# Scores of odd heads in banks of their own, in the single-piece steps of a causal attention

## The chip, the cores and the metric

The kernel runs on the 8 cores of one Trainium2 chip. Each core computes 2 of the 16 sequences of the batch, with all weights, and the cores exchange nothing. The metric is the device time in microseconds (us) of the slowest core.

## What is computed

One pre-norm transformer block: causal attention with 16 heads of 64, then a gated feed-forward part with two hidden 4096 x 4096 layers. Per core 2 sequences of 2048 tokens, width 1024.

```python
# x: (16, 2048, 1024), layernorm without gain and bias
qkv  = jnp.einsum('btc,hdc->bhtd', layernorm(x), w_qkv); q, k, v = jnp.split(qkv, 3, axis=-1)
dots = jnp.einsum('bhtd,bhsd->bhts', q, k) * hs ** (-0.5)
dots = jnp.where(causal, dots, -jnp.inf)
out  = jnp.einsum('bhts,bhsd->bhtd', jax.nn.softmax(dots, axis=-1), v)
x = x + out.transpose(0, 2, 1, 3).reshape(Bx, Tx, -1) @ w_proj.T + b_proj
y = layernorm(x)
h = silu((y @ w1.T) * w1_s) * ((y @ w2.T) * w2_s)
h = gelu((h @ h1.T) * h1_s);  h = gelu((h @ h2.T) * h2_s)
x = x + (h @ w3.T) * w3_s
```

## The kernel before

Each core runs attention for its first sequence, then for its second, then four feed-forward sweeps of 1024 tokens. Every instruction is put into one of five engine queues when the program is built. An engine works through its queue in order. An instruction carries the semaphore values that it waits for. On VectorE and ScalarE each instruction also waits for the one before it on the same engine.

**Attention** of one sequence: layernorm and transposes of 16 token tiles (lines 310 to 360), projections to Q, K and V for eight pairs of heads (L401 to L434), and then the steps: 16 query tiles of 128 queries (`qt`) times 16 heads (`h_`), heads innermost. A step of query tile `qt` has K = (qt+1)·128 keys. PSUM has 8 banks of 512 fp32 columns. Banks 0 to 3 take the scores, in pieces of 1024 columns (two banks), banks 4 and 5 the transposed probabilities, banks 6 and 7 the output of all heads of a tile. Query tiles 0 to 7 have up to 1024 keys and so one piece ("single-piece"), tiles 8 to 15 have two.

The parts of a step:

- `emit_qpad`: ScalarE copies the head's 64 rows of Q into one of two zero-padded buffers (L464), by the parity of the head.
- `emit_S_mm`: PE computes the scores, one matmul per 512 keys (L490). VectorE takes the negated maximum of a full first piece (L499, two-piece steps only), adds the causal mask to the last 128 columns (L504), takes the negated maximum of the last piece (L509), and joins the two (L513, two-piece only).
- `emit_exps`: ScalarE writes the exponential to SBUF with a running sum (L530, ACTIVATE and the read of the accumulator). VectorE copies the sum (L547), or adds the two of a two-piece step (L543). `gbank` of the score banks is set to the exponential: it is what the next score matmul into the bank waits for. `expg[par]` does the same for mask and maximum, by the parity of the head.
- `emit_PTAV`: for each group of four key blocks of 128, PE transposes the probabilities into bank 4 or 5 (L566). ScalarE (even groups, L576) or VectorE (odd groups, L579) copies them to SBUF, and PE multiplies them with V (L593). Steps of up to 512 keys have one group, those of 640 to 1024 keys two.
- `emit_tail`: after the last head of a query tile, scaling (L611, L618), transposes (L626), the output projection (L643), bias and residual (L652, L655) and the store.

The order of the emission is one head ahead: scores, mask and maximum of step i, the Q copy of step i+1, transposes and AV of step i-1 (and the tail, if that was the tile's last head), then the exponential of step i:

```python
for idx, (qt, h_) in enumerate(seq):
    nmx, vred = emit_S_mm(qt, h_)
    if idx + 1 < len(seq):
        emit_qpad(*seq[idx + 1])
    if pend is not None:
        emit_PTAV(*pend)
        if pend[1] == H - 1:
            emit_tail(pend[0])
    cev_ = emit_exps(qt, h_, nmx, vred)
```

So PE's queue holds scores of i, transposes of i-1, AV of i-1, scores of i+1. VectorE's holds mask and maximum of i, the L579 copy of i-1, L547 of i, mask of i+1. ScalarE's holds the Q copy for i+1, the L576 copy of i-1, the exponential of i.

**The feed-forward sweeps**: each has the gate and up matmuls (L767, 1024 of 512 columns), two hidden layers (L812, 2048 matmuls each) and the output layer (L851), with the weights streamed in from scratch copies in HBM that GpSimd's queue cast to bf16 during the first attention.

Of the kernel before, what the change touches and what calls it, by code (L numbers as in the profile page):

```python
# [69 lines left out]
def ceil_div(a, b):  # L70
    return (a + b - 1) // b


def build(cfg):
# [108 lines left out]
    PS = ps_t.ap()  # L183

    def sb(off, n, dtype=BF16, parts=(0, 128)):
        if dtype == BF16:
            v = A[parts[0]:parts[1], off // 2: off // 2 + n]
        else:
            v = A[parts[0]:parts[1], off // 2: off // 2 + 2 * n].bitcast(F32)
        return v  # L190

    def bank(i, w=512):
        return PS[:, i * 512: i * 512 + w]
# [5 lines left out]
    mtri = sb(o_binT, 128)  # L199
# [24 lines left out]
    s_exp = s_wt = s_e  # L224
    prog.self_sem = {"vector": v_e, "scalar": s_e}

    gbank = {i: None for i in range(8)}
    tw_lane = [0, 0]

    def em(eng, fn, wait=(), inc=None, inc_n=1):  # L230
        return prog.emit(eng, fn, wait, inc, inc_n)
# [134 lines left out]
    def attention(b):  # L366
# [15 lines left out]
        for hp in range(NHP):  # L382
# [9 lines left out]
            for part, dsto, evac_eng in ((0, o_Q, "scalar"), (1, o_K, "vector")):  # L392
                for tt in range(NT5):
                    bk = part * 2 + (tt % 2) if False else (0 if part == 0 else 1)
                    bk = (tt % 2) + (0 if part == 0 else 2)
                    for cc in range(NCC):
# [5 lines left out]
                               o, l, r, start=st_, stop=sp),  # L402
# [15 lines left out]
            for sc_ in range(T // 128):  # L418
                bk = 4 + (sc_ % 2)
                for cc in range(NCC):  # L420
# [5 lines left out]
                           o, l, r, start=st_, stop=sp),  # L426
# [41 lines left out]
        def emit_S_mm(qt, h_):  # L468
            K_ = (qt + 1) * 128
            npiece = ceil_div(K_, 1024)  # L470
            qtw = qt * 128
            pd = qtw // 1024
            hp, lo = h_ // 2, (h_ % 2) * 64
            hpv = hp * T
            par = h_ % 2
            nm = sb(o_nmp + par * 16, 4, F32)
            qp = (o_qpad // 2) + par * 128
            qpad_ev = qpad_evs[par]
            ts_p = []
            for p in range(npiece):  # L480
                w_p = min(1024, K_ - p * 1024)
                for jj in range(ceil_div(w_p, 512)):
                    w_j = min(512, w_p - jj * 512)
                    bk = 2 * p + jj
                    off = p * 1024 + jj * 512
                    lhs = A[:, qp: qp + 128]
                    rhs = A[:, (o_K // 2) + hpv + off:
                            (o_K // 2) + hpv + off + w_j]
                    em("tensor", lambda t, o=bank(bk, w_j), l=lhs, r=rhs:
                       t.matmul(o, l, r, start=True, stop=True),  # L490
                       wait=(gbank[bk], qpad_ev,
                             qkv_done_v if qt == 0 and h_ == 0 else None,
                             qkv_done_s if qt == 0 and h_ == 0 else None),
                       inc=t_s if jj == ceil_div(w_p, 512) - 1 else None)
                ts_p.append((t_s, t_s.v))
                if p < pd:
                    em("vector", lambda v, o=nm[:, p:p + 1],
                       i_=PS[:, p * 1024: p * 1024 + 1024]:
                       v.tensor_reduce(out=o, in_=i_, axis=AX.X, op=ALU.max,  # L499
                                       negate=True),  # L500
                       wait=(ts_p[p], expg[h_ % 2]))
            qpad_guard[par] = (t_s, t_s.v)
            em("vector", lambda v, o=PS[:, qtw: qtw + 128], m=mtri:
               v.tensor_tensor(out=o, in0=o, in1=m, op=ALU.add),  # L504
               wait=(ts_p[pd], expg[h_ % 2]))
            w_pd = K_ - pd * 1024
            em("vector", lambda v, o=nm[:, pd:pd + 1],
               i_=PS[:, pd * 1024: pd * 1024 + w_pd]:
               v.tensor_reduce(out=o, in_=i_, axis=AX.X, op=ALU.max,  # L509
                               negate=True))  # L510
            if npiece > 1:
                em("vector", lambda v, o=nm[:, 3:4], i_=nm[:, 0:npiece]:
                   v.tensor_reduce(out=o, in_=i_, axis=AX.X, op=ALU.min,  # L513
                                   negate=False))
            nmx = nm[:, 3:4] if npiece > 1 else nm[:, 0:1]
            return nmx, (v_e, v_e.v)

        def emit_exps(qt, h_, nmx, vred):
            K_ = (qt + 1) * 128
            nsc = qt + 1  # L520
            par = h_ % 2
            Poff = (o_P // 2) + par * T
            rsp = sb(o_rsp + par * 16, 4, F32)
            nj = ceil_div(K_, 1024)
            chunk_ev = {}
            for j in range(nj):
                w_j = min(1024, K_ - j * 1024)
                em("scalar", lambda sc, o=A[:, Poff + j * 1024: Poff + j * 1024 + w_j],
                   i_=PS[:, j * 1024: j * 1024 + w_j], bi=nmx, a=rsp[:, j:j + 1]:
                   sc.activation(out=o, in_=i_, func=AF.Exp, bias=bi, scale=1.0,  # L530
                                 accum_out=a),
                   wait=(vred, hpar_guard[par] if j == 0 else None,
                         rsg[par] if j == 0 else None),
                   inc=s_exp)
                for sc_ in range(j * 8, min(j * 8 + 8, nsc)):
                    chunk_ev[sc_] = (s_exp, s_exp.v)
                gbank[2 * j] = (s_exp, s_exp.v)
                gbank[2 * j + 1] = (s_exp, s_exp.v)
            expg[par] = (s_exp, s_exp.v)
            rs = sb(o_rs, H, F32)  # L540
            if nj > 1:
                em("vector", lambda v, o=rs[:, h_:h_ + 1], i_=rsp[:, 0:nj]:
                   v.tensor_reduce(out=o, in_=i_, axis=AX.X, op=ALU.add),  # L543
                   wait=(expg[par],), inc=v_e)
            else:
                em("vector", lambda v, o=rs[:, h_:h_ + 1], i_=rsp[:, 0:1]:
                   v.tensor_copy(o, i_), wait=(expg[par],), inc=v_e)  # L547
            rsg[par] = (v_e, v_e.v)
            return chunk_ev
# [126 lines left out]
# [9 lines that stand above are left out]
            pend = (qt, h_, cev_)  # L685
# [311 lines left out]
```

How the kernel before makes its waits and increments, by code:

```python
def build(cfg):  # L74
# [830 lines left out]
    gbank[("xF", 1)] = x1_stores_done  # L905
    gbank[("x2F", 0)] = x1_stores_done
    gbank[("x2F", 1)] = x1_stores_done
    t0 = 0
    for si, SW in enumerate(sweeps):
        ffn_sweep(si, t0, SW)
        t0 += SW
    final_st = d_st.v
    em("sync", lambda s: s.wait_ge(d_st.h, final_st))
    with nc.Block() as block:
        def run(eng_name):
            def _(eng):
                for waits, fn, inc, inc_n in prog.q[eng_name]:
                    for s, v in waits:
                        eng.wait_ge(s.h, v)
                    inst = fn(eng)
                    if inc is not None:
                        inst.then_inc(inc.h, inc_n)
```

## Time and profile before

| | |
|---|---|
| median of 3 runs | 8859.74 us (8769.2 to 9204.07) |
| profiled execution | 8801.45 us |
| span of its slowest core (core 2) | 8799.8 us |
| spans of the others | 8734.7 to 8790.0 us |
| PE, DVE, ACT busy | 79%, 20%, 23% of the span |
| mean granted TensorE clock, core 2 | 0.834 |
| attention of the first and second sequence | to about 1848 and 3493 us, the rest is feed-forward |

Times in the rows are us from the span's start. PE is TensorE's matmuls, PEld its weight loads, DVE VectorE, ACT ScalarE, POOL GpSimd. The granted clock (PEclk) is a share of 2.4 GHz, so 0.50 is 1.2 GHz. L490 is line 490 of the kernel. All rows are of core 2.

### The profile page before, as it was taken

The numbers are of one execution on the slowest core, as the hardware profiler recorded it, in microseconds if no ns is written. First come the engines' busy times: TensorE is split into PE (matmuls) and PEld (weight loads), VectorE is DVE, ScalarE is ACT, GpSimd is POOL, SyncE is SP. The second block draws the span as 40 slices with busy tenths as digits, with TensorE's granted clock in tenths as the row PEclk, the third lists the DMA queues.
The fourth block names the chain that finished last, engine by engine and source line by source line (L and its number), as shares of the span: only waits on it lengthen the run. The fifth ranks groups of instructions, "written<-read, shape, count | busy, mean of one in ns | idle before, by whom it ended". The sixth has DMA issues, their size and how long they took to land.

```text
span 8799.8 us, 101925 instructions; the slowest of 8 cores (8734.7 to 8799.8 us)
## 1 busy us (share of the span) xinstructions
PE 6972.6 (79%) x37120; PEld 3410.8 (39%) x37120; DVE 1802.5 (20%) x3585; ACT 2024.7 (23%) x3840; POOL 191.9 (2%) x142
## 2 busy tenths in 40 slices
PE   0645556657455665999997999996999996999998
PEld 0423333334233333444443444443444443444443
DVE  1234445543344455200000200001200001100000
ACT  0034455532445554210000210000210000110000
POOL 1000000100000000000000000000000000000000
PEclk9965555668555565999998999998999998899999
DMA  5987777531000000333336333335333335333335
GB/s 78 94 83 76 77 72 73 57 61 26 20 15 11 10 11 22 77 79 76 76 77 140 73 79 77 77 76 140 71 78 77 77 77 139 59 77 76 76 77 129
DMA packets 2139544, 626.25 MB, mean 71 GB/s; under 512 B 2114224, under 2 KB 2114352, under 8 KB 2139056
## 3 DMA queue, kind: packets, MB, share of 16 engines
q1 hardware_dynamic: 1649184, 417.41, 23.7%
q0 software_dynamic: 461216, 101.00, 13.4%
q10 hardware_dynamic: 28656, 101.34, 3.5%
q8 instruction: 306, 5.01, 0.3%
q14 instruction: 182, 1.49, 0.1%
HBM read 269.23 MB, written 134.22 MB: 46 GB/s over the span
## 4 chain that ended last, share of the span: by engine, by line
PE 67%; DVE 12%; issue 7%; DMA 7%; ACT 6%; DVEq 1%; ACTq 1%; SPq 0%; POOLq 0%
PE ps L812 40%; PE ps L767 11%; PE ps L851 4%; PE ps L490 4%; DVE arena L509 4%; ACT arena L530 4%; PE ps L401 3%; DVE arena L499 2%; DMA arena<-x_scratch 2%; PE ps L643 2%; DMA qkvB<-wqkv 2%; DVE ps L504 1%; ACT arena L576 1%; DMA arena<-w3B 1%; PE ps L566 1%
## 5 line engine op out<-in xcount | busy, mean ns | idle before, releaser
L812 PE MATMUL ps<-arena 128*128 128x512 bf16 x16384 | 3537.5, 379 | 9.0 <-DVE arena L790 5.1
L812 PEld LDWEIGHTS ps<-arena 128*128 128x128 bf16 x16384 | 1602.6, 98 | 1944.0 <-issue 12.7
L825 ACT ACTIVATE arena<-ps,arena 128x512 bf16<-128x512 f32 x512 | 351.7, 687 | 3158.8 <-PE ps L812 3158.8
L593 PE MATMUL ps<-arena 128*128 128x64 bf16 x4352 | 402.6, 228 | 719.2 <-DVE arena L579 400.4
L767 PE MATMUL ps<-arena 128*128 128x512 bf16 x4096 | 930.4, 393 | 0.0
L885 DVE TENSOR_TENSOR arena<-ps,arena 128x1024 f32<-128x1024 f32 x32 | 39.2, 1224 | 4155.8 <-DMA arena<-x_scratch 4155.8
L490 PE MATMUL ps<-arena 128*128 128x512 bf16 (+3 forms) x1280 | 541.1, 531 | 351.0 <-ACT arena L530 347.5
L530 ACT ACTIVATE arena<-ps,arena 128x1024 bf16<-128x1024 f32 (+7 forms) x768 | 663.9, 864 | 439.9 <-DVE arena L655 259.5
L593 PEld LDWEIGHTS ps<-arena 128*128 128x128 bf16 x4352 | 268.8, 115 | 927.7 <-issue 927.3
L566 PE MATMUL ps<-arena 128*128 128x128 bf16 x4352 | 624.4, 305 | 0.0
L767 PEld LDWEIGHTS ps<-arena 128*128 128x128 bf16 x4096 | 411.7, 101 | 517.2 <-issue 141.0
L576 ACT COPY arena<-ps 128x512 bf16<-128x512 bf16 (+3 forms) x768 | 408.3, 532 | 783.8 <-PE ps L566 783.8
L566 PEld LDWEIGHTS ps<-arena 128*128 128x128 bf16 x4352 | 476.0, 142 | 142.5 <-issue 130.8
L851 PE MATMUL ps<-arena 128*128 128x512 bf16 x2048 | 455.8, 384 | 18.0 <-DMA arena<-w3B 14.0
L509 DVE TENSOR_REDUCE arena<-ps 128x1 f32<-128x512 f32 (+7 forms) x512 | 388.0, 758 | 54.8 <-DVE ps L504 1.6
L790 DVE SCALAR_TENSOR_TENSOR arena<-ps,arena 128x512 bf16<-128x512 f32 x256 | 192.1, 751 | 746.8 <-PE ps L767 746.8
L783 ACT ACTIVATE arena<-ps,arena 128x512 bf16<-128x512 f32 x256 | 175.9, 687 | 726.0 <-PE ps L767 725.5
L348 PE MATMUL ps<-arena 128*128 128x128 bf16 x512 | 63.3, 307 | 350.8 <-DVE arena L339 327.5
L401 PE MATMUL ps<-arena 128*128 128x512 bf16 x1024 | 227.8, 384 | 142.0 <-DMA arena<-qkvB 140.7
L499 DVE TENSOR_REDUCE arena<-ps 128x1 f32<-128x1024 f32 x256 | 313.5, 1224 | 62.3 <-PE ps L490 47.9
L490 PEld LDWEIGHTS ps<-arena 128*128 128x128 bf16 x1280 | 102.3, 106 | 572.1 <-issue 567.7
L851 PEld LDWEIGHTS ps<-arena 128*128 128x128 bf16 x2048 | 200.5, 99 | 272.1 <-issue 50.2
(51 smaller groups left out, 2371.4 us busy)
## 6 DMA issues: line engine op xcount, KB each, us to landing
arena<-x ACTq DMA_DIRECT2D x64, 512.0 KB, 4.5
h1B<-h POOLq DMA_DIRECT2D x32, 1024.0 KB, 16.3
h2B<-h POOLq DMA_DIRECT2D x32, 1024.0 KB, 15.9
arena<-x_scratch ACTq DMA_DIRECT2D x64, 512.0 KB, 4.2
x_scratch<-arena ACTq DMA_DIRECT2D x32, 512.0 KB, 2.8
out<-arena ACTq DMA_DIRECT2D x32, 512.0 KB, 3.0
w1B<-w POOLq DMA_DIRECT2D x8, 1024.0 KB, 18.8
w2B<-w POOLq DMA_DIRECT2D x8, 1024.0 KB, 16.1
```

Of the source, the lines that this page charges most:

```text
L401: st_=(cc == 0), sp=(cc == NCC - 1): t.matmul(o, l, r, start=st_, stop=sp),
L490: t.matmul(o, l, r, start=True, stop=True),
L499: v.tensor_reduce(out=o, in_=i_, axis=AX.X, op=ALU.max, negate=True),
L509: v.tensor_reduce(out=o, in_=i_, axis=AX.X, op=ALU.max, negate=True))
L530: sc.activation(out=o, in_=i_, func=AF.Exp, bias=bi, scale=1.0, accum_out=a),
L566: em("tensor", lambda t, o=outb, i_=inb: t.transpose(o, i_, ident), wait=(chunk_ev[sc_] if (idx == 0 or sc_ == qt) else None, gbank[("pt", ...
L576: em("scalar", lambda sc, d=dstv, s=srcv: sc.copy(d, s), wait=(tpt, gbank[("PT", slot)]), inc=csem)
L593: st_=(sc_ == 0), sp=(sc_ == nsc - 1): t.matmul(o, l, r, start=st_, stop=sp),
L767: st_=(cc == 0), sp=(cc == NCC - 1): t.matmul(o, l, r, start=st_, stop=sp),
L812: st_=(dc == 0), sp=(dc == ND - 1): t.matmul(o, l, r, start=st_, stop=sp),
L825: s1=scalev[:, oc:oc + 1]: sc.activation(out=o, in_=i_, func=AF.Gelu, scale=s1),
L851: st_=(dc == 0), sp=(dc == ND - 1): t.matmul(o, l, r, start=st_, stop=sp),
```

## The change

In single-piece steps the scores of odd heads go to PSUM columns 1024 to 2047 (banks 2 and 3), those of even heads stay in columns 0 to 1023 (banks 0 and 1). The offset `sbase` is added where the scores are written, masked, reduced, exponentiated, and where the bank guards are set. In two-piece steps `sbase` is 0 and nothing changes. No instruction is added or removed, and the order of the queues is the same.

```diff
@@ emit_S_mm
+            sbase = par * 1024 if npiece == 1 else 0
             ...
-                    bk = 2 * p + jj
+                    bk = sbase // 512 + 2 * p + jj
             ...
-                       i_=PS[:, p * 1024: p * 1024 + 1024]:
+                       i_=PS[:, sbase + p * 1024: sbase + p * 1024 + 1024]:
             ...
-            em("vector", lambda v, o=PS[:, qtw: qtw + 128], m=mtri:
+            em("vector", lambda v, o=PS[:, sbase + qtw: sbase + qtw + 128], m=mtri:
             ...
-               i_=PS[:, pd * 1024: pd * 1024 + w_pd]:
+               i_=PS[:, sbase + pd * 1024: sbase + pd * 1024 + w_pd]:
@@ emit_exps
+            sbase = par * 1024 if nj == 1 else 0
             ...
-                   i_=PS[:, j * 1024: j * 1024 + w_j], bi=nmx, a=rsp[:, j:j + 1]:
+                   i_=PS[:, sbase + j * 1024: sbase + j * 1024 + w_j], bi=nmx,
+                   a=rsp[:, j:j + 1]:
             ...
-                gbank[2 * j] = (s_exp, s_exp.v)
-                gbank[2 * j + 1] = (s_exp, s_exp.v)
+                gbank[sbase // 512 + 2 * j] = (s_exp, s_exp.v)
+                gbank[sbase // 512 + 2 * j + 1] = (s_exp, s_exp.v)
```

## Rows read from the trace of the kernel before

**Rows 1.** The page, part 4: the chain that ended last, by line.
```profile
PE ps L812 40%; PE ps L767 11%; PE ps L851 4%; PE ps L490 4%; DVE arena L509 4%; ACT arena L530 4%; PE ps L401 3%; DVE arena L499 2%; DMA arena<-x_scratch 2%; PE ps L643 2%; DMA qkvB<-wqkv 2%; DVE ps L504 1%; ACT arena L576 1%; DMA arena<-w3B 1%; PE ps L566 1%
```

**Rows 2.** Groups by line and shape, 0 to 3600 us: busy us, mean ns | idle before.
```profile
L547 DVE COPY arena<-arena 128x1 f32<-128x1 f32 x256 | 39.4, 154 | 254.3 <-ACT arena L530 249.0 <-ACT arena L464 5.3
...
L579 DVE COPY arena<-ps 128x128 bf16<-128x128 bf16 x64 | 14.4, 224 | 28.1 <-PE ps L566 24.8
```

**Rows 3.** Timeline, one step with 1024 keys: start, us, engine line operation [idle before].
```profile
940.82 1.11 ACT L530 ACTIVATE arena<-ps,arena 128x1024 bf16<-128x1024 f32 x1 [0.74 <-DVE arena L509]
...
942.17 1.01 PE L490 MATMUL ps<-arena 128*128 128x512 bf16 x2 [0.45 <-ACT arena L530]
942.19 0.15 DVE L547 COPY arena<-arena 128x1 f32<-128x1 f32 x1 [1.00 <-ACT arena L530]
...
942.98 1.06 PE L566 MATMUL ps<-arena 128*128 128x128 bf16 x8
...
943.36 0.30 DVE L504 TENSOR_TENSOR ps<-ps,arena 128x128 f32<-128x128 f32 x1 [1.01 <-PE ps L490]
943.76 1.23 DVE L509 TENSOR_REDUCE arena<-ps 128x1 f32<-128x1024 f32 x1
943.81 0.58 ACT L576 COPY arena<-ps 128x512 bf16<-128x512 bf16 x1 [1.40 <-PE ps L566]
...
945.09 0.42 DVE L579 COPY arena<-ps 128x512 bf16<-128x512 bf16 x1
945.13 1.11 ACT L530 ACTIVATE arena<-ps,arena 128x1024 bf16<-128x1024 f32 x1 [0.74 <-DVE arena L509]
...
945.66 0.37 PE L593 MATMUL ps<-arena 128*128 128x64 bf16 x4 [0.75 <-DVE arena L579]
```

**Rows 4.** Timeline, one step with 256 keys.
```profile
529.37 0.47 ACT L530 ACTIVATE arena<-ps,arena 128x256 bf16<-128x256 f32 x1 [0.37 <-DVE arena L509]
...
530.08 0.37 PE L490 MATMUL ps<-arena 128*128 128x256 bf16 x1 [0.66 <-ACT arena L530]
...
530.11 0.15 DVE L547 COPY arena<-arena 128x1 f32<-128x1 f32 x1 [0.89 <-ACT arena L530]
...
530.63 0.30 DVE L504 TENSOR_TENSOR ps<-ps,arena 128x128 f32<-128x128 f32 x1 [0.37 <-PE ps L490]
...
531.03 0.42 DVE L509 TENSOR_REDUCE arena<-ps 128x1 f32<-128x256 f32 x1
...
531.61 0.47 ACT L530 ACTIVATE arena<-ps,arena 128x256 bf16<-128x256 f32 x1 [0.36 <-DVE arena L509]
```

**Rows 5.** Windows: busy us (instructions) by engine, PEclk, DMA share, GB/s.
```profile
901.00:966.00 65.00, 38.37 (x262) 22.84 (x262) 30.55 (x59) 31.28 (x60) 6.31 (x4) 0.50 0.76 73
...
1520.00:1580.00 60.00, 39.17 (x310) 23.26 (x308) 33.48 (x69) 36.03 (x69) 6.31 (x4) 0.61 0.66 59
```

**Rows 6.** Timeline, end of a step of the last, two-piece query tile.
```profile
1776.12 1.11 ACT L530 ACTIVATE arena<-ps,arena 128x1024 bf16<-128x1024 f32 x1
...
1776.57 0.37 PE L593 MATMUL ps<-arena 128*128 128x64 bf16 x4 [0.53 <-DVE arena L579]
...
1776.76 1.47 PE L490 MATMUL ps<-arena 128*128 128x512 bf16 x3
```

**Rows 7.** Timeline, L547 in another step with 256 keys.
```profile
523.38 0.15 DVE L547 COPY arena<-arena 128x1 f32<-128x1 f32 x1 [1.24 <-ACT arena L464]
```

**Rows 8.** The chain of work in order of time, attention's end: start, us, what.
```profile
3492.64 2.61 DMA x_scratch<-arena
3495.79 6.45 DMA arena<-x_scratch
```

**Rows 9.** The chain, L767 of the third and fourth sweep, and a window in the latter.
```profile
6168.66 222.05 PE ps L767 x1024
...
7487.00 262.71 PE ps L767 x1024
...
7507.00:7527.00 20.00, 20.00 (x78) 8.30 (x77) 3.00 (x4) 3.73 (x6) 0.00 (x0) 0.81 0.33 66
```

## Prediction

> **What bounds the kernel now.** I read the page's chain of work first: the feed-forward line L812 holds 40% of it, and the lines of the softmax steps (L490, L509, L530, L499) about 4%, 4%, 4% and 2% [rows 1]. The change touches only those, so it works inside the attention part, and there only in the steps of the first eight query tiles, whose scores fit into two PSUM banks. The grouped view gives their number: L547 runs in these steps alone, 256 times (8 tiles x 16 heads x 2 batches) [rows 2]. The same row shows VectorE idle for 254.3 us ahead of it, 249.0 us of that until the exponential of the same head was done.
>
> Then I read the timeline of single steps, one large and one small. With 1,024 keys a step repeats every 4.31 us (940.82 to 945.13). The reader should follow one chain through it: exponential L530 starts at 940.82; its accumulator is read out 1.35 us later and at 942.17 the two score matmuls L490 start on the banks just freed; the mask add L504 starts 1.19 us after them, the maximum L509 0.40 us after that, runs 1.23 us, and the next exponential starts 0.14 us behind it [rows 3]. With 256 keys it is the same chain: 0.71 + 0.55 + 0.40 + 0.58 = 2.24 us (529.37 to 531.61) [rows 4]. No engine is full; a ring of waits through ACT, PE and DVE sets the pace. The granted clock is 0.50 in such a stretch, which is the level of 1.2 GHz [rows 5].
>
> **The change, part by part.** Nothing is computed more or less, no DMA is touched, no wait is added. Odd heads of single-piece steps put their scores at column 1,024 of PSUM, so in banks 2 and 3, and mask, maximum and exponential follow. The guard of the score matmul of head h+1 becomes the exponential of head h-1, long done, instead of that of head h. The bookkeeping costs nothing: every instruction keeps its size and engine. What is worth time is how early L490 of head h+1 can start now, and what is late next. All queues keep their order, so two waits take over.
>
> The first is on VectorE. Its queue holds, between the maximum of head h and the mask of head h+1, the copy L547, which waits for the exponential of head h. Mask and maximum therefore can't run beside that exponential; only the score matmul can. Before, L547 started 0.02 to 0.03 us after L490 (942.19 against 942.17, 530.11 against 530.08). After, the mask starts behind L547: its 0.15 us and 0.11 us from one VectorE instruction's end to the next one's start (943.76+1.23 to 945.09 shows 0.10) [rows 3, 4]. The stretch from L490 to L504 (1.19 us with 1,024 keys, 0.55 with 256) shrinks to 0.02 or 0.03 + 0.26. That saves 0.91 and 0.26 us. Between them it grows by (1.19-0.55)/6 = 0.107 us for each 128 keys. I call this loop B. Its savings by keys, 128 to 1,024: 0.16, 0.26, 0.37, 0.48, 0.58, 0.69, 0.80, 0.91.
>
> The Trainium skill (PSUM — Partial Sum Buffer, section Engine vs sequencer instructions) says that the VectorE and ScalarE queues are strictly first in, first out. It speaks against reading the change as full overlap of two heads, and the trace agrees, with 249.0 us of such waiting at L547. Could the mask pass L547, at most 0.26 us more would be saved in each of the 128 steps of up to 512 keys, 33 us, and the time would be 8655.
>
> The second wait exists from 640 keys on, where a step has a second group of transposes. Its copy L579 is on VectorE behind the maximum, the AV matmuls L593 wait for the copy, and L490 of the next head is behind these on PE. Loop C with 1,024 keys: 0.10 from the maximum's end to L579 (944.99 to 945.09), 0.42 copy, 0.15 to L593 (945.51 to 945.66), then L593 to L490, 1.19 to the mask, 0.40 to the maximum, 1.23 maximum [rows 3]. L593 to L490 doesn't occur unblocked in these steps. The nearest row is in the last tile of the batch: L593 at 1776.57, L490 at 1776.76, so 0.19 us [rows 6]. Bounds: 0, since it can't start ahead of it; and 0.37 + 0.15 = 0.52, if it waited for L593's end (0.37) and one hand-over more. I take 0.19, as it is the same pair of lines. Loop C is 3.68 us then, against 4.31: 0.63 saved, less than loop B's 0.91, so C decides. With 640 keys: the step before is 2.24 + 3 x 0.345 = 3.28 (0.345 is (4.31-2.24)/6); C is 0.10 + 0.22 + 0.15 + 0.19 + 0.87 + 0.40 + 0.83 = 2.76, with the copy from the grouped rows [rows 2] and the maximum between 0.42 and 1.23 [rows 3, 4]; 0.52 saved, under B's 0.58. Between them 0.55 and 0.59.
>
> ScalarE has a ring of its own: exponential, transposes, copy L576, next exponential. With 512 keys: 0.92 us to the transposes (between 0.71 and 1.35), 0.83 to the copy (942.98 to 943.81), 0.58 copy, 0.10 to the next: 2.43 [rows 3, 4]. The step in loop B is 2.24 + 2 x 0.345 - 0.48 = 2.45. It lies just behind and doesn't decide.
>
> Sum for the eight tiles: 0.16 + 0.26 + 0.37 + 0.48 + 0.52 + 0.55 + 0.59 + 0.63 = 3.56 us per head; x 16 heads x 2 batches = 114 us. That takes the step across a tile's end (projection, residual) for one like the others: the score matmul of the next tile's first head is moved in the same way. Nothing catches up the gain: the chain goes from the last tile's store to the loads of the feed-forward part, with no wait for weights between [rows 8]. The profiled execution took 8801.45 us; 8801.45 - 114 = 8687. This execution lies between the runs shown (8769.2 and the median 8859.74), so a median may come out up to 50 us higher.
>
> Bounds of the sum: with 0.52 for L593 to L490 each large step saves 0.33 less: 64 x 2 x 0.33 = 42 us, so 72 us and 8729. With 0 each large step saves 0.19 more, capped by loop B: 1.27 + 0.58 + 0.69 + 0.78 + 0.82 = 4.14 us, x 32 = 132 us, 8669.
>
> **Rivals.** *The clock rises.* PE's work of a step would stand closer together. In a stretch of the later tiles, where it does so too, the granted clock is 0.61, so partly the level of 2.4 GHz [rows 5]. At that level L490 and the transposes halve, loop C drops below B, and B holds everywhere: 4.25 x 32 = 136 us, 8665. Against it: most of that stretch stays at 1.2 GHz as well, and all of the one with 1,024 keys. The Trainium skill (TensorE: Matmul & The Clock Gate, Part 1) says that the gate follows how busy PE has been, two levels and none between; the mean of 0.61 fits a mixture.
>
> *A late release takes the place.* L547 now is on the path, and it isn't always let go at once: at 523.38 VectorE had been idle for 1.24 us ahead of it, where the regular step has 0.89 [rows 4, 7]. Before, the score matmul hid this. If each step lost these 0.35 us, loop B would save 0, 0, 0.02, 0.13, 0.23, 0.34, 0.45, 0.56: 1.73 x 32 = 55 us, 8746. Against it: almost all of the steps in the trace are regular.
>
> *It doesn't do what it says.* PE now writes scores while ScalarE reads the other head's. If the exponential were held up for as long as the matmul streams (0.107 us per 128 columns, 36 x 0.107 = 3.85 us over the eight sizes), of loop B's 4.25 us only 0.40 x 32 = 13 us would be left: 8788. Against it: in a two-piece step the exponential of 1776.12 takes 1.11 us with L490 of 1776.76 beside it, as long as the one of 940.82 with no L490 beside it [rows 3, 6].
>
> *Slower than before: the granted clock of the feed-forward part.* On core 2 the L767 stage took 222.05 us in the third sweep and 262.71 in the fourth, whose stretch from 7507 shows a granted clock of 0.81 [rows 9]. Place: the dense matmul stages, which the change shifts in time against those of the other cores. Price: 40.7/222 = 18% of each stage so affected. It decides from 114/0.18 = 620 us of such stages more than now. If one sweep's three long stages fell into it (222 us and two of the eight L812 stages, which share 40% of the span, so 440 us each [rows 1, 9]), that is 1102 us and 18% of it: 8687 + 202 = 8889. Against it: one stage of a fourth of the sweeps shows it, and nothing ties it to attention. The Trainium skill (same page, Part 1) describes a current limit of a die at 13/16 of the clock for as long as dense load lasts; the level agrees with 0.81, the stages at full clock do not.
>
> **How the numbers follow.** Forecast (rings B and C) 0.60, the clock rises 0.10, a late release 0.17, doesn't do what it says 0.06, the feed-forward clock 0.07. The predicted time is 8687, of the first alone 8669 to 8729. The range of 8640 to 8790 takes in the first four and some of the spread of runs on both sides; outside are the last and an execution far from the profiled one. About 2% (176 us) is what a measurement of this kernel can tell from no change. Faster by more needs all rings at their upper bound and 40 us from elsewhere: 0.04. Slower by more needs 290 us of loss: 0.03. Within: 0.93.
>
> **What would show it.** Steps with 256 keys at 1.98 us, with 1,024 at 3.68; L490 starting before its neighbour's exponential ends, 0.19 us behind L593 in the large steps; L504 idle until L547 in the small ones; L530 at 1.11 us as before; L812's stages unchanged. I am wrong on the size if L593 to L490 is longer, on the mechanism if L504 doesn't follow L547 below 640 keys, and on the whole if exponentials get longer.

## The result and the profile after

The changed kernel is faster. The ratio of its time to that of the kernel before is 0.983, with a 95% interval of 0.978 to 0.988; the median of its ten executions is 8656.36 us. Measured twice more, the ratio was 0.985 (0.978 to 0.992) and 0.989 (0.975 to 1.004). Ratios leave out executions that a lower granted clock made more than about 1% slower, so the first compares the means of six executions after (8650.96 us) and three before (8799.82 us), and what is left still differs by up to 1.3% within one kernel. The quickest executions of the three comparisons differ by 121.7, 113.5 and 101.5 us; in the second they are 8741.73 us before (8747.71 the next) and 8628.27 after (8632.21 the next), so 113 us, or 1.3%.

That the feed-forward part takes the same time in both kernels where its granted clock doesn't dip can be seen in the chains of two cores without such a dip. Core 5 of the kernel before, the chain of work in order of time (start, us, what):

```profile
3526.36 221.52 PE ps L767 x1024
3749.11 442.20 PE ps L812 x2048
...
7464.24 222.06 PE ps L767 x1024
```

Core 5 of the changed kernel, measured again; the lines of the same stages are L770 and L815 there:

```profile
3414.91 221.75 PE ps L770 x1024
3637.89 442.20 PE ps L815 x2048
...
7353.17 222.10 PE ps L770 x1024
```

From the first gate matmul to the end of the span core 5 needs 8734.7 - 3526.4 = 5208.3 us before and 8622.8 - 3414.9 = 5207.9 us after (the spans by core say 8734.7 and 8622.8). In this pair all 111.4 us were gone before the feed-forward part began. The six cores without a dip in the trace before need 5208 to 5214 us for this part, and the sixteen of the changed kernel's two further traces 5206 to 5222. The 111.4 itself is one pair's: within one execution the first gate matmul of the eight cores lies between 3526 and 3558 us before, and between 3399 and 3416 us in the changed kernel measured again. What the change touches is steadier. The 128 single-piece steps of a sequence and the tile ends between them, from the first exponential to the first of the ninth tile, both sequences added, take 1015.6 us before on the mean of the cores, 898.5 in the changed kernel and 896.3 when measured again: 117 and 119 us less.

The step with 1024 keys, which [rows 3] show before. Changed kernel, core 4, timeline (start, us, engine line operation [idle before]). Here and in the timelines below the rows of PE's weight loads are left out without a mark. L490 is now L491, mask L504 is L505, maximum L509 is L510, L530 is L533, L547 is L550, L566 is L569, L576 is L579, L579 is L582, L593 is L596:

```profile
847.63 0.42 DVE L582 COPY arena<-ps 128x512 bf16<-128x512 bf16 x1
847.68 1.11 ACT L533 ACTIVATE arena<-ps,arena 128x1024 bf16<-128x1024 f32 x1 [0.74 <-DVE arena L510]
848.20 0.37 PE L596 MATMUL ps<-arena 128*128 128x64 bf16 x4 [0.75 <-DVE arena L582]
848.38 1.04 PE L491 MATMUL ps<-arena 128*128 128x512 bf16 x2
...
849.05 0.15 DVE L550 COPY arena<-arena 128x1 f32<-128x1 f32 x1 [1.00 <-ACT arena L533]
849.22 1.06 PE L569 MATMUL ps<-arena 128*128 128x128 bf16 x8
849.60 0.30 DVE L505 TENSOR_TENSOR ps<-ps,arena 128x128 f32<-128x128 f32 x1 [0.40 <-PE ps L491]
850.00 1.22 DVE L510 TENSOR_REDUCE arena<-ps 128x1 f32<-128x1024 f32 x1
...
851.33 0.42 DVE L582 COPY arena<-ps 128x512 bf16<-128x512 bf16 x1
851.38 1.11 ACT L533 ACTIVATE arena<-ps,arena 128x1024 bf16<-128x1024 f32 x1 [0.74 <-DVE arena L510]
```

It repeats every 3.70 us instead of 4.31. The score matmul starts at 848.38, while the exponential of 847.68 still runs, and directly behind the AV matmuls of 848.20. This is loop C: copy 847.63, AV 848.20, scores 848.38, mask 849.60, maximum 850.00, copy 851.33. The exponential is 1.11 us long, as before, though for 0.41 us of it PE writes the other head's scores.

The step with 256 keys, which [rows 4] show before, on the same core:

```profile
504.24 0.37 PE L569 MATMUL ps<-arena 128*128 128x128 bf16 x2 [0.40 <-ACT arena L533]
504.26 0.15 DVE L550 COPY arena<-arena 128x1 f32<-128x1 f32 x1 [0.88 <-ACT arena L533]
504.52 0.30 DVE L505 TENSOR_TENSOR ps<-ps,arena 128x128 f32<-128x128 f32 x1
...
504.92 0.42 DVE L510 TENSOR_REDUCE arena<-ps 128x1 f32<-128x256 f32 x1
...
505.40 0.40 PE L491 MATMUL ps<-arena 128*128 128x256 bf16 x1
505.50 0.47 ACT L533 ACTIVATE arena<-ps,arena 128x256 bf16<-128x256 f32 x1 [0.32 <-DVE arena L510]
```

The score matmul of the next head starts before the exponential does (505.40 and 505.50), where it waited for that exponential's end before. The mask stands directly behind L550, whose idle time ends with the exponential. This is loop B.

The grouped rows of core 4 say the same in sums (busy us, mean ns | idle before); those of the kernel before are first, those of the changed kernel second:

```profile
L490 PE MATMUL ps<-arena 128*128 128x256 bf16 x128 | 51.5, 402 | 28.4 <-ACT arena L530 28.4
```

```profile
L491 PE MATMUL ps<-arena 128*128 128x256 bf16 x128 | 52.4, 409 | 0.0
L550 DVE COPY arena<-arena 128x1 f32<-128x1 f32 x256 | 39.4, 154 | 254.4 <-ACT arena L533 249.1 <-ACT arena L464 5.3
```

With 256 keys PE no longer waits for the exponential ahead of the scores. VectorE waits as long as it did ahead of the sum copy: 254.4 us, 254.3 in [rows 2].

### The profile page after: what moved, and what is told of

Read it like the earlier page. It is cut to its first block, busy times and chain, and to the rows that moved or that the text cites. A ratio compares the mean times of both kernels' runs of the same rounds, so it can differ in the third digit from the quotient of the medians.

```text
span 8770.9 us, 101927 instructions; the slowest of 8 cores (8634.0 to 8770.9 us)
## 1 busy us (share of the span) xinstructions
PE 7022.5 (80%) x37120; PEld 3399.8 (39%) x37120; DVE 1803.4 (21%) x3585; ACT 2025.9 (23%) x3840; POOL 192.4 (2%) x142
## 4 chain that ended last, share of the span: by engine, by line
PE 68%; DVE 12%; DMA 7%; issue 6%; ACT 6%; DVEq 1%; ACTq 1%; POOLq 0%; SPq 0%
PE ps L815 41%; PE ps L770 10%; PE ps L854 4%; DVE arena L510 4%; ACT arena L533 4%; PE ps L491 3%; PE ps L401 3%; DVE arena L500 2%; DMA arena<-x_scratch 2%; PE ps L646 2%; DMA qkvB<-wqkv 2%; DVE ps L505 1%; ACT arena L579 1%; PE ps L596 1%; PE ps L569 1%
## 5 line engine op out<-in xcount | busy, mean ns | idle before, releaser
L815 PE MATMUL ps<-arena 128*128 128x512 bf16 x16384 | 3634.3, 386 | 8.9 <-DVE arena L793 5.0
L815 PEld LDWEIGHTS ps<-arena 128*128 128x128 bf16 x16384 | 1625.2, 99 | 2018.1 <-issue 331.1
L596 PE MATMUL ps<-arena 128*128 128x64 bf16 x4352 | 401.6, 227 | 719.8 <-DVE arena L582 401.3
L770 PE MATMUL ps<-arena 128*128 128x512 bf16 x4096 | 907.0, 386 | 0.0
L533 ACT ACTIVATE arena<-ps,arena 128x1024 bf16<-128x1024 f32 (+7 forms) x768 | 664.5, 865 | 432.7 <-DVE arena L658 249.9
L569 PE MATMUL ps<-arena 128*128 128x128 bf16 x4352 | 613.0, 302 | 104.6 <-ACT arena L533 100.8
L491 PE MATMUL ps<-arena 128*128 128x512 bf16 (+3 forms) x1280 | 546.8, 536 | 145.2 <-ACT arena L533 141.7
L596 PEld LDWEIGHTS ps<-arena 128*128 128x128 bf16 x4352 | 268.2, 115 | 925.1 <-issue 924.4
L770 PEld LDWEIGHTS ps<-arena 128*128 128x128 bf16 x4096 | 406.2, 99 | 499.2 <-issue 62.8
L579 ACT COPY arena<-ps 128x512 bf16<-128x512 bf16 (+3 forms) x768 | 409.3, 533 | 671.3 <-PE ps L569 671.2
L569 PEld LDWEIGHTS ps<-arena 128*128 128x128 bf16 x4352 | 451.3, 138 | 291.1 <-issue 280.3
L854 PE MATMUL ps<-arena 128*128 128x512 bf16 x2048 | 452.1, 382 | 19.1 <-DMA arena<-w3B 12.6
L510 DVE TENSOR_REDUCE arena<-ps 128x1 f32<-128x512 f32 (+7 forms) x512 | 388.1, 758 | 54.8 <-DVE ps L505 1.6
L401 PE MATMUL ps<-arena 128*128 128x512 bf16 x1024 | 228.1, 384 | 148.8 <-DMA arena<-qkvB 147.5
L491 PEld LDWEIGHTS ps<-arena 128*128 128x128 bf16 x1280 | 109.8, 112 | 333.3 <-issue 325.7
```

The source lines that it names most:

```text
L401: st_=(cc == 0), sp=(cc == NCC - 1): t.matmul(o, l, r, start=st_, stop=sp),
L510: v.tensor_reduce(out=o, in_=i_, axis=AX.X, op=ALU.max, negate=True))
L569: em("tensor", lambda t, o=outb, i_=inb: t.transpose(o, i_, ident), wait=(chunk_ev[sc_] if (idx == 0 or sc_ == qt) else None, gbank[("pt", ...
L579: em("scalar", lambda sc, d=dstv, s=srcv: sc.copy(d, s), wait=(tpt, gbank[("PT", slot)]), inc=csem)
L596: st_=(sc_ == 0), sp=(sc_ == nsc - 1): t.matmul(o, l, r, start=st_, stop=sp),
L770: st_=(cc == 0), sp=(cc == NCC - 1): t.matmul(o, l, r, start=st_, stop=sp),
```

## The experiments

Two questions were open. First, are the two rings what holds a step, size by size? Second, does the ratio of 0.983 hold more than the 114 us of the rings? Below, "step" is the median distance between the starts of two exponentials of one size, over the 15 distances of the first sequence. "Stretch" is the time of all single-piece steps and tile ends in both sequences as defined above, the mean of the eight cores.

**The changed kernel again, twice.**

> The changed kernel once more, to settle its size. Ring theory (all of the gain is the earlier score matmul in the 256 single-piece steps, 0.16, 0.26, 0.37, 0.48, 0.58, 0.64, 0.63, 0.61 us by size, less some 10 us at the tile ends): about 110 us less on undisturbed cores, 8650 against 8765, a ratio of 0.987, with the same stage times in the feed-forward part. Rival (the change also brings the feed-forward part to a better clock): a ratio of 0.983 or less, about 150 us, also on cores whose granted clock is undisturbed.

> The changed kernel a third time, beside the two above. Ring theory: 113 us less than the kernel before on undisturbed cores, ratio 0.987. Rival (a better clock in the feed-forward part belongs to the change): 0.983 or less.

Measured: 8628.27 us at best against 8741.73, ratio 0.985; then 8643.97 against 8745.44, ratio 0.989 with an interval that takes in 1. The steps were 1.73, 1.97, 2.21, 2.45, 2.69, 2.98, 3.34 and 3.70 us in both. The ring theory holds; on the rival the feed-forward times of the section above decide. Whether a quicker attention part makes such dips in the feed-forward part rarer stays open: the comparisons hold too few executions to tell.

**Only the four smallest tiles, only the four largest.**

```diff
-            sbase = par * 1024 if npiece == 1 else 0
+            sbase = par * 1024 if qt < 4 else 0                     # the small ones
+            sbase = par * 1024 if npiece == 1 and qt >= 4 else 0    # the large ones
```

(and the same in `emit_exps`.)

> Odd heads in banks of their own only in the four smallest query tiles (128 to 512 keys). Ring theory: these save 0.16 + 0.26 + 0.37 + 0.48 = 1.27 us per head, 41 us in all, about 8725, and their steps repeat at 1.73, 1.97, 2.21, 2.45 us; the other four stay at 3.27 to 4.31 us. Rival (a released matmul is worth something only where it is long): well under 20 us.

> Odd heads in banks of their own only in the tiles of 640 to 1024 keys. Ring theory: 2.46 us per head, 79 us less some at the tile ends, about 8690, steps at 2.69, 2.98, 3.34, 3.70 us, the small ones at 1.89 to 2.93 as before. The two halves should add up to the whole change (41 + 79). Rival (the halves share a limit): the sum of both differs from the whole by more than 20 us.

Measured on the same chip, best executions: 8702.05 us for the small ones, 39.7 less than before, with steps of 1.73, 1.97, 2.21, 2.45 and then 3.27 to 4.31; 8663.51 for the large ones, 78.2 less, with steps of 1.89 to 2.93 and then 2.69, 2.98, 3.34, 3.70. The halves sum to 118 us, the whole gave 113. The ratio of the large half is 0.991 (0.983 to 0.998); the time of the small half is that of a single execution, and there is no ratio. The stretches are the firmer evidence: 41 us less in the small half and 76 in the large one, together the 117 of the whole. The halves don't share a limit, and both terms of the sum are the size they were given.

**The row sum later.** VectorE's copy L547 of each single-piece step is put behind mask and maximum of the next head.

```diff
             nmx, vred = emit_S_mm(qt, h_)
+            while rs_late:
+                emit_rs(*rs_late.pop(0))
...
-            em("vector", ... v.tensor_copy(o, i_), wait=(expg[par],), inc=v_e)
+            rs_late.append((h_, nj, rsp, expg[par], par))
```

> The changed kernel, with the VectorE copy of the row sum moved behind mask and maximum of the next head in single-piece steps; same instructions, other order. Theory (VectorE's queue order is what holds the mask: loop B): the steps up to 640 keys fall further, from 1.73, 1.97, 2.21, 2.45, 2.69 to about 1.44, 1.75, 2.08, 2.40, 2.60 us, where ScalarE's ring takes over; the larger ones stay, held by loop C. 25 us less than the change, about 8625. Rival (the exponential itself or the accumulator read holds the next mask): no step changes, 8650.

> The kernel before, all heads in banks 0 and 1, with the copy of the row sum moved behind mask and maximum of the next head in single-piece steps. Theory (before the change the score matmul waits for the exponential, and the copy is hidden beside it): no change, steps at 1.89 to 4.31 us, 8765. Rival (the copy's place in VectorE's queue is the limit in itself, banks or not): up to 0.26 us less in each of 256 steps, 67 us.

Measured on the changed kernel: the four small sizes fell to 1.43, 1.75, 2.07, 2.39 us, as expected. The four large ones rose, to 2.88, 3.24, 3.60, 3.96, which was not expected; the time was the same as the change's (8626.95 against 8628.27), and so was the stretch (898.5 us). On the kernel before no step moved; the ratio is 1.003 (0.998 to 1.008), the stretch 1020.5 us, 5 more than before. So the place of L547 is the limit of the small steps, and it is so only since the banks are apart. The miss shows in the timeline of a step with 1024 keys (core 0; L559 is the sum copy, L590 the copy of the transposed probabilities, L604 AV):

```profile
852.55 1.22 DVE L510 TENSOR_REDUCE arena<-ps 128x1 f32<-128x1024 f32 x1
...
853.87 0.15 DVE L559 COPY arena<-arena 128x1 f32<-128x1 f32 x1
853.92 1.11 ACT L533 ACTIVATE arena<-ps,arena 128x1024 bf16<-128x1024 f32 x1 [0.74 <-DVE arena L510]
854.13 0.42 DVE L590 COPY arena<-ps 128x512 bf16<-128x512 bf16 x1
854.70 0.37 PE L604 MATMUL ps<-arena 128*128 128x64 bf16 x4 [1.00 <-DVE arena L590]
854.89 1.04 PE L491 MATMUL ps<-arena 128*128 128x512 bf16 x2
```

The sum copy now stands between maximum and copy, in the middle of loop C: 853.87 to 854.13 are the 0.26 us by which 3.70 became 3.96.

**The row sum behind that copy.** The same, but emitted after `emit_PTAV`.

```diff
             nmx, vred = emit_S_mm(qt, h_)
-            while rs_late:
-                emit_rs(*rs_late.pop(0))
...
             if pend is not None:
                 emit_PTAV(*pend)
+                while rs_late:
+                    emit_rs(*rs_late.pop(0))
```

> As the late row sum, but placed behind VectorE's copy of the transposed probabilities instead of ahead of it (single-piece steps). Theory for the miss of the late sum (its 0.15 + 0.11 us stood between maximum and copy, so inside loop C, and made the large steps 0.2 to 0.26 us longer): the small steps stay at 1.43, 1.75, 2.07, 2.39 us, and the large ones go to about 2.60, 2.98, 3.34, 3.70 us, 25 us less than the change. Rival (the large steps became longer for another reason, such as contention of earlier masks): 2.88 to 3.96 us again.

Measured: 1.43, 1.75, 2.07, 2.39, 2.62, 2.98, 3.34, 3.70 us, at best 8604.48 us against 8745.44 before on that chip, 141 less. The large steps are back at the change's, so loop C and the place in it are confirmed. With 640 keys, where loop C lies below B, the step falls from 2.69 to 2.62.

**Scores ahead of the last AV matmuls.** In tiles of 640 to 1024 keys PE gets the score matmuls of head h+1 before the last AV group of head h-1.

```diff
+            if nxt is not None and qt >= 4 and nxt[0] < 8:
+                ts_n = []
+                S_matmuls(nxt[0], nxt[1], ts_n, None)
+                ahead[nxt] = ts_n[0]
             emit_AV(ngrp - 1)
```

> The changed kernel, with the score matmuls of the next head ahead of the last AV matmuls on PE, in tiles of 640 to 1024 keys; same instructions. Theory (from 768 keys on loop C holds: maximum, copy, AV, score matmul): steps fall to loop B, from 2.98, 3.34, 3.70 to 2.92, 3.17, 3.41 us, 640 keys stays at 2.69; 17 us less than the change, about 8633. Rival (PE or VectorE is simply full there): no change.

Measured: 2.69, 2.93, 3.17, 3.41 us for the four large sizes, to 0.01 us what loop B gives, and the small ones untouched; at best 8616.41 us against 8745.08 before, ratio 0.982 (0.975 to 0.989), stretch 884.7 us. With 1024 keys the score matmul (L489 here) now starts ahead of VectorE's copy L601 (core 0):

```profile
852.13 0.37 PE L615 MATMUL ps<-arena 128*128 128x64 bf16 x4 [0.51 <-ACT arena L598]
852.31 1.04 PE L489 MATMUL ps<-arena 128*128 128x512 bf16 x2
852.62 0.42 DVE L601 COPY arena<-ps 128x512 bf16<-128x512 bf16 x1
852.67 1.11 ACT L552 ACTIVATE arena<-ps,arena 128x1024 bf16<-128x1024 f32 x1 [0.69 <-DVE arena L529]
...
854.05 0.15 DVE L569 COPY arena<-arena 128x1 f32<-128x1 f32 x1 [1.00 <-ACT arena L552]
854.30 0.30 DVE L524 TENSOR_TENSOR ps<-ps,arena 128x128 f32<-128x128 f32 x1
```

The mask L524 stands directly behind the sum copy L569 again: loop C is gone and B holds.

**Both together**, with the row sum ahead of the copy and then behind it. The first moves the row sum in the two-piece steps too, the second in the single-piece steps only.

> Both: early score matmuls and the late row sum (the latter in two-piece steps as well). Theory: loops B and C are both gone and ScalarE's ring (exponential, transposes, copy, exponential) holds all eight sizes: about 1.44, 1.75, 2.08, 2.40, 2.54, 2.65, 2.76, 2.86 us. With 1024 keys that is 0.84 less than the change, where each alone gives 0 and 0.29: 83 us less than the change in all, about 8565, more if two-piece steps gain. Rival (a limit of another kind, such as VectorE's total, lies right behind): no better than the sum of the two, about 42 us less.

> Early score matmuls and the row sum behind the copy, in single-piece steps. ScalarE's ring should hold all eight sizes: 1.43, 1.75, 2.07, 2.39, 2.54, 2.65, 2.76, 2.86 us, less where the granted clock rises; some 80 us less than the change, about 8555 on undisturbed cores. Rival (VectorE's order still holds the largest): 896 and 1024 keys stay at 2.97 us as in the run with both, 60 us less.

Measured: at best 8584.06 us against 8745.08 for the first, ratio 0.984 (0.976 to 0.992), and 8568.83 against 8745.44 for the second. The last is 176.6 us or 2.0% less than the kernel before, ratio 0.980 (0.968 to 0.991), so it is the quickest of all. Its stretch is 823.6 us, 192 less than before. The row sum's move in the two-piece steps was a loss: from the ninth tile's first exponential to the last tile's last one, a sequence took 853 to 854 us, and 841 to 847 in the kernel before and in the second.

The medians are 1.43, 1.75, 2.07, 2.39, 2.50, 2.74, 2.97, 2.97 us in the first, and the same to 0.01 in the second on seven cores. Up to 640 keys the expectation holds. From 768 keys on the steps alternate and a median is only the longer of two: on core 2 of the second kernel 2.60 and 2.75 us with 768 keys, 2.71 and 2.99 with 896, and with 1024 for most of the tile 2.82 and 3.23. Means of such pairs are 2.68, 2.85 and 3.02, where 2.65, 2.76 and 2.86 were expected, so from 896 keys on ScalarE's ring is not what holds them. VectorE's sum copy isn't either: its place differs in the two kernels and the steps don't. Two steps with 1024 keys on that core:

```profile
833.73 0.59 ACT L606 COPY arena<-ps 128x512 bf16<-128x512 bf16 x1 [0.64 <-PE ps L596]
834.46 0.37 PE L623 MATMUL ps<-arena 128*128 128x64 bf16 x4 [0.51 <-ACT arena L606]
834.64 1.04 PE L489 MATMUL ps<-arena 128*128 128x512 bf16 x2
834.79 0.42 DVE L609 COPY arena<-ps 128x512 bf16<-128x512 bf16 x1
834.84 1.11 ACT L552 ACTIVATE arena<-ps,arena 128x1024 bf16<-128x1024 f32 x1 [0.52 <-DVE arena L529]
...
835.86 0.30 DVE L524 TENSOR_TENSOR ps<-ps,arena 128x128 f32<-128x128 f32 x1 [0.39 <-PE ps L489]
836.13 0.30 ACT L464 COPY arena<-arena 64x128 bf16<-64x128 bf16 x1
836.19 1.01 PE L596 MATMUL ps<-arena 128*128 128x128 bf16 x8 [0.29 <-ACT arena L552]
836.26 1.22 DVE L529 TENSOR_REDUCE arena<-ps 128x1 f32<-128x1024 f32 x1
836.98 0.59 ACT L606 COPY arena<-ps 128x512 bf16<-128x512 bf16 x1 [0.55 <-PE ps L596]
...
837.65 1.11 ACT L552 ACTIVATE arena<-ps,arena 128x1024 bf16<-128x1024 f32 x1
...
837.71 0.37 PE L623 MATMUL ps<-arena 128*128 128x64 bf16 x4 [0.51 <-ACT arena L606]
...
837.89 1.04 PE L489 MATMUL ps<-arena 128*128 128x512 bf16 x2
...
839.11 0.30 DVE L524 TENSOR_TENSOR ps<-ps,arena 128x128 f32<-128x128 f32 x1 [0.84 <-PE ps L489]
839.51 1.22 DVE L529 TENSOR_REDUCE arena<-ps 128x1 f32<-128x1024 f32 x1
...
840.88 1.11 ACT L552 ACTIVATE arena<-ps,arena 128x1024 bf16<-128x1024 f32 x1 [0.51 <-DVE arena L529]
```

The mask waits 0.39 us for the score matmul L489, which stands behind the first AV group, which waits for ScalarE's copy L606, and that for transposes and exponential of the head before. This ring goes over two heads: exponential to transposes 1.35, to the copy 0.79, to AV 0.73, to scores 0.18, to the mask 1.22, to the maximum 0.40, to the next but one exponential 1.37, in all 6.04 us or 3.02 for each step. That is also the distance between the exponentials of 834.84 and 840.88, whose two steps are 2.81 and 3.23. An estimate from the same rows, with 0.107 us less to the transposes, 0.107 less to the mask and 0.134 less for the maximum for each 128 keys fewer, gives 5.69 and 5.34 us for two steps of 896 and 768 keys; measured are 5.70 and 5.35. Where the granted clock is higher the steps are shorter: on core 4 2.61 and 2.71 us alternate from 848 us on, with a granted clock of 0.90 between 846 and 857 us. The reading is from the rows; no run took this ring away.

## Why the prediction was right or wrong

**The sum was right.** Forecast were 114 us less, 8687 from the profiled 8801.45; the stretch of the single-piece steps became 117 to 119 us shorter, and the best executions of the three comparisons differ by 101 to 122 us. The median of 8656.36 lies inside the range, 31 us under the forecast. The profiled execution was not an undisturbed one: the 262.71 us of L767 in [rows 9] alone hold 40.7 us over the stage of the third sweep. I had read that row, and used it for a rival only, not for the base of the sum. So the base was too high, and the predicted time with it. Against 8769.2, the lowest time shown, 114 less would have been 8655: the 31 us are the base's, and not those of a ring.

**The conclusion from the sum was wrong.** The failing step is in how the numbers follow: "About 2% (176 us) is what a measurement of this kernel can tell from no change", with 0.93 within. That threshold was put there without a row or a run behind it, and it turned a forecast gain of 1.3% into no change. The runs showed a finer resolution: six of the ten executions of the changed kernel lie between 8647.54 and 8657.89 us, 0.12% apart, and the first ratio is known to 0.5% either way (0.978 to 0.988), or some 45 us. The first two comparisons have intervals that leave out 1 on the side of faster; the third, with two executions after in it, takes in 1. The forecast should have been called faster and small. The ratio of 0.983 reads larger than 1.3% because the execution of 8859.74 us is one of only three in its denominator; without it the means give 0.986. That the time lies in the range says little: a base 32 us too high fitted into its 150 us as well.

**The terms.** Loop B: 1.73, 1.98, 2.21, 2.45 us were forecast and 1.73, 1.97, 2.21, 2.45 measured. Loop C: 2.76, 3.07, 3.38, 3.68 were forecast and 2.69, 2.98, 3.34, 3.70 measured. At 1024 keys L593 to L490 took 0.18 us against the 0.19 that I took (848.20 to 848.38). From 640 to 896 keys the term was too large, since the 0.19 came from a group of four AV matmuls and these have one to three in their last group. At 640 loop C then falls below B: 2.69 is B's value, as the run with early scores shows, where 640 keys didn't move, and without B the step was 2.62. By size the steps save 0.16, 0.26, 0.37, 0.48, 0.58, 0.64, 0.63, 0.61 us, 3.73 against the forecast 3.56.

**The step across a tile's end** was counted as one like the others. The eight distances of the first sequence sum to 133.5 us before and 132.3 after on core 0, and to 135.8 and 131.3 on core 4; over the eight cores the mean falls from 134.6 to 131.5 in the first sequence, so 3.1 saved and not 3.7, and from 134.5 to 130.5 in the second sequence, where 4.0 are saved. With the steps that is 15 x 2 x 3.73 + 3.1 + 4.0 = 119 us. Irregular steps take back a little: with means in place of medians the eight sizes save 3.68, and the stretches show 117 to 119. How much of that reaches the end isn't known to some 10 us, as the best executions (101 to 122 us) and the start of the feed-forward part show: on the mean of the cores it came 104 us earlier in one execution and 132 in another.

**The rivals.** The clock did not rise: the mean granted clock of each of the eight tiles is 0.50 to 0.54 in both kernels, so nearly all at 1.2 GHz. Only in the last two kernels did it rise in part, to a mean of 0.59 to 0.73 in the tile of 1024 keys. The late release is there, but rare: on core 4 two steps of 15 with 256 keys took 2.32 and 2.26 us instead of 1.97. A hindered exponential is excluded by its 1.11 us. The feed-forward clock is the scatter of both kernels, not an effect of the change that could be shown. Of the Trainium skill's rule on first-in, first-out queues (PSUM — Partial Sum Buffer, section Engine vs sequencer instructions) this case's runs agree: moving one copy of 0.15 us in VectorE's queue changed the steps by up to 0.30 us one way and up to 0.26 the other. I had put what is to be had from passing L547 at 33 us at most, 0.26 in each of the small steps; with the copy behind L579 these fell by 0.30, 0.22, 0.14 and 0.06 us, which is 23 us in all, and 25 with the 0.07 at 640 keys. The stretch, which holds the irregular steps too, is 866.1 us, 29 to 32 less than the change's, and the best execution 39.5 less than the change's on the same chip (8604.48 and 8643.97).

## What to carry to other kernels

When a buffer is doubled to break a ring of waits, write down the next ring for each size before the run: which instruction stands in the in-order queue between the freed one and its user, and what that one waits for. Here a copy of one column, free for as long as the ring ran over PE, was worth up to 0.30 us a step afterwards, and it cost up to 0.26 us when it was moved to a place that looked free. Look at single steps and not only at their median: a ring over two heads shows as two alternating lengths. Check the base of a sum for stages that are longer than their repeats, and take the smallest gain that can be told from none out of the scatter of the runs, before a computed 1.3% is called no change.

## What was not expected of the hardware

A PE instruction that needs nothing starts before the one ahead of it has ended, by the trace's modelled ends: scores 0.18 us behind the start of four AV matmuls of 0.37 us, and 0.06 us behind the weight load of the single last AV matmul with 640 keys (649.81 to 649.87 on core 4). One step from VectorE's maximum to its next instruction is 0.10 us, from VectorE to PE 0.15 us. These two hand-overs are the same to 0.01 us in nearly every step of the three traces of the changed kernel, so a ring's length could be forecast to 0.02 us where each of its rows was in the trace.
